# Exponentials and maxima on crossed score banks: VectorE and ScalarE change places halfway

## The chip, the cores and the metric

One core of one Trainium2 chip runs the whole kernel. The metric is the device time in microseconds of one execution, and the time of a kernel is the median of its runs.

## The reference, cut to what matters

A gated block over x of 128 sequences of 64 tokens with 128 channels: a cross attention with 16 heads of 8 channels, and a feed-forward network whose tokens are routed to one of 8 experts. The change lies in the attention's softmax.

```python
def _L0_xattn_ref(q, k, v, W_q, b_q, W_k, b_k, W_v, b_v, W_o, b_o):
    qh = _split_heads(q @ W_q + b_q)
    kh = _split_heads(k @ W_k + b_k)
    vh = _split_heads(v @ W_v + b_v)
    scores = jnp.einsum('bhqd,bhkd->bhqk', qh, kh) / jnp.sqrt(jnp.asarray(D_K, qh.dtype))
    probs = jax.nn.softmax(scores, axis=-1)
    ctx = jnp.einsum('bhqk,bhkd->bhqd', probs, vh)
    ...
x = x + jnp.tanh(g_xattn[0]) * _L0_xattn_ref(_layernorm(x), ctx_1024, ctx_1024, ...)
x = x + jnp.tanh(g_ffn[0]) * _L0_ffn_ref(_layernorm(x), ...)
```

## The kernel before, in words

The attention is a pipeline written out by hand. A unit is 128 tokens (two sequences); there are 64 units (NU), and four of them share a load, a projection and a turn of the inputs. One loop over slots k = 0 to 75 stands in each engine's program, and in slot k every engine does the stages of several units at once: scores for the maxima of unit k-4 (LAG1), scores for the exponential of unit k-10 (LAG2), values of unit k-11 (LAGV), output projection of unit k-12 (LAGO). With j = k % 4 and s = k // 4, every fourth slot has the same extra work. The engines meet only through semaphores.

The scores stand in one PSUM tile sc of four banks, one bank for each of four groups of heads (t). Columns 0 to 255 of each bank hold the scores that VectorE takes the maxima of (bf16 products, `scores1`, L1162 to L1170), columns 256 to 511 those that ScalarE exponentiates (float32 products from which the maxima of that earlier pass have been taken away by the matmul of MD and usel, `scores2`, L1143 to L1160). There is one sc, so a slot's scores can be written only after the slot before has been read: `scores(k)` waits for pt_ok (the exponentials of the slot before) and mx_ok (its maxima), `peaks(k)` for mx_ok.

TensorE's order in a slot is: scores2 (L1150, L1157), scores1 (L1167), values (L1232, which wait for nv_ok of the unit before), output projection (L1244, which waits for ot_ok), and then what j asks for: in slot j = 0 four transposes of x (L1319), four of the context (L1266), two small ones (L1325, L1327); in j = 1 the keys (L1273); in j = 2 logits (L1256) and queries (L1337, called the wqp matmul); in j = 3 logits and the V projection (L1344).

VectorE's order in a slot is: two reductions of the maxima (L1012), the first over banks 0 and 1 (signals mxa_ok), the second over banks 2 and 3 (mx_ok); the transpose TV (L1021, waits for pv_ps, which the output projection of the slot signals), the residual (L1000), reciprocal (L1027), a statistic (L735), NV (L1032, signals nv_ok), another statistic (L727), the transpose OT (L1039, ot_ok), in j = 1 also L740 and the logits (L811), and in most of the slots from 24 on a step of the routing.

ScalarE's order in a slot is: the two exponentials (L614 over banks 0 and 1, L616 over banks 2 and 3, which signals pt_ok), then the copies that j asks for (j = 0: xT L629, cT L575, mS L663; j = 1: kb L581 and two kT L588; j = 2: qb L644, Qf L647; j = 3: two V copies L656 and xwT L668), and last the squares of the residual (L543, an activation and a read of its accumulator). The first exponential waits for s2_ps (its scores), mxa_ok and pv_ps (its output buffer), the second for mx_ok. So the two engines pass through the banks in one order, ScalarE one step behind VectorE, and never read one bank at the same time.

A second loop of 71 tiles runs the experts behind the attention; nothing in it is touched.

Of the kernel before, what the change touches and what calls it, by code (L numbers as in the profile page):

```python
# [6 lines left out]
ACT = mybir.ActivationFunctionType  # L7
# [16 lines left out]
NU = N // P  # L24
# [16 lines left out]
LAG1, LAG2, LAGV, LAGO = 4, 10, 11, 12  # L41
# [22 lines left out]
def gated_block(nc, x, ctx_in, g_xattn, g_ffn, W_q, b_q, W_k, b_k, W_v, b_v, W_o, b_o, w_red, wg, W1, b1, W2, b2, out):  # L64
    es = ExitStack()
    with es:
# [3 lines left out]
        def pb(name, shape, dt=F32):  # L70
            return es.enter_context(nc.psum_tensor(name, shape, dt))

        def sem(name):
            return es.enter_context(nc.semaphore(name))
# [93 lines left out]
        sc = pb("sc", [P, RT, 512])  # L168
# [22 lines left out]
        qd_in = [sem(f"qd_in{i}") for i in range(3)]  # L191
        md_ok = sem("md_ok")
        imask_ok, par_ok, bkp_ok = sem("imask_ok"), sem("par_ok"), sem("bkp_ok")
        s1_ps, mxa_ok, mx_ok, mT_ps, mS_ok, s2_ps, pt_ok = (sem(n) for n in ("s1_ps", "mxa_ok", "mx_ok", "mT_ps", "mS_ok", "s2_ps", "pt_ok"))
        pv_ps, val_ps, tv_ok, rec_ok, nv_ok, ot_ok, x1_ok = (
            sem(n) for n in ("pv_ps", "val_ps", "tv_ok", "rec_ok", "nv_ok", "ot_ok", "x1_ok"))
        gsq_ok, gve_ok, g_pay, xw_ps, xwT_ok, xwt_ps, lgx_ok = (
# [13 lines left out]
        def pv_turn(k):  # L211

            return k - LAGV + 1
# [280 lines left out]
        def _(act):  # L494
# [8 lines left out]
            def permuted(w, wp):  # L503
                nc.scalar.activation(wp[:, :].rearrange("p (t d i) -> p t d i", t=RT, d=DK),
                                     w[:, :].rearrange("p (t i d) -> p t d i", t=RT, d=DK), ACT.Copy).then_inc(perm_ok, 1)

            def permuted_biases():
                for i in range(2):
                    b_ = nc.scalar.activation(browp[:, i, :].rearrange("o (t d i) -> o t d i", t=RT, d=DK),
                                              brow[:, i, :].rearrange("o (t i d) -> o t d i", t=RT, d=DK), ACT.Copy)  # L510
                b_.then_inc(brow_ok, 1)
# [3 lines left out]
            def bias_columns():  # L515
                act.wait_ge(bcol_ps, 1)
                nc.scalar.mul(b16[:, 0:1], m2[:, 0:1], ISC)
                nc.scalar.activation(b16[:, 1:2], m2[:, 1:2], ACT.Copy).then_inc(b16_ok, 1)
                act.wait_ge(b16_ok, 1)
                act.wait_ge(par_ok, 1)  # L520
                nc.scalar.activation(bkp[:, :], par[:, :], ACT.Copy, scale=b16[:, 1:2]).then_inc(bkp_ok, 1)
                act.wait_ge(bkp_ok, 1)
# [33 lines left out]
            def gate_weights_end():  # L556
                act.wait_ge(wc_ps, 1)
                nc.scalar.activation(wc[:, 0:NE], m2[:, 0:NE], ACT.Copy).then_inc(wc_ok, 1)

            def turned_weights():  # L560

                act.wait_ge(wt_ps, 1)
                nc.scalar.activation(wt[:, :, :].rearrange("p a c -> p (a c)"), pv[:, P:3 * P], ACT.Copy).then_inc(wt_ok, 1)
# [7 lines left out]
            def turned_context(s):  # L571
                act.wait_ge(cT_ps, s + 1)
                if s >= 1:
                    act.wait_ge(v_ps, s)
                nc.scalar.activation(cT[:, :], m1[:, :], ACT.Copy).then_inc(cT_sb, 1)  # L575
# [29 lines left out]
            for k in range(SLOTS):  # L605
                s, j = k // CU, k % CU
                n = k - LAG2
                if 0 <= n < NU:
                    act.wait_ge(s2_ps, n + 1)
                    act.wait_ge(mxa_ok, min(k - LAG1 + 1, NU))  # L610
                    if n >= 2:
                        act.wait_ge(pv_ps, pv_turn(n - 2 + LAGV))
                    pt = PT[n % 2][:, :, :].rearrange("p (t i) q -> p t (i q)", t=RT)
                    nc.scalar.activation(pt[:, 0:2], sc[:, 0:2, 256:512], ACT.Exp)  # L614
                    act.wait_ge(mx_ok, min(k - LAG1 + 1, NU))
                    nc.scalar.activation(pt[:, 2:4], sc[:, 2:4, 256:512], ACT.Exp).then_inc(pt_ok, 1)  # L616
                if k == 7:
                    gate_weights_end()
                if k == 0:
                    turned_context(0)  # L620
                    permuted(wq, wqp)
                    permuted_biases()
                    bias_columns()
                    keys(0)
                if j == 0 and s < NC:
                    act.wait_ge(xT_ps, s + 1)
                    if s >= 2:
                        act.wait_ge(xw_ps, s - 1)
                    nc.scalar.activation(xT[s % 2][:, :], m0[:, :], ACT.Copy).then_inc(xT_sb, 1)  # L629
                if k == 0:  # L630
                    keys_turned(0)
                    act.wait_ge(w_in, 16 * NWI)
                    nc.scalar.activation(tg[:, :], gx[:, :], ACT.Tanh)
                    nc.scalar.activation(tgf[:, :], gf[:, :], ACT.Tanh).then_inc(tg_ok, 1)
                if j == 0 and 1 <= s < NC:
                    turned_context(s)
                if j == 1 and 1 <= s < NC:
                    keys(s)
                    keys_turned(s)
                if j == 2 and s < NC:  # L640
                    act.wait_ge(q_ps, s + 1)
                    if s >= 2:
                        act.wait_ge(s1_ps, CU * (s - 1))
                    nc.scalar.activation(qb[s % 2][:, :], m0[:, :], ACT.Identity, bias=b16[:, 0:1], scale=ISC).then_inc(qb_ok, 1)  # L644
                    if s >= 1:
                        act.wait_ge(qd_in[(s - 1) % 3], 16 * HI * ((s - 1) // 3 + 1))
                    nc.scalar.activation(Qf[:, :], m0[:, :], ACT.Identity, bias=b16[:, 0:1], scale=ISC).then_inc(qf_ok, 1)  # L647
                if j == 3 and s < NC:
                    act.wait_ge(v_ps, s + 1)
                    if s < 3:  # L650
                        act.wait_ge(zero_p, s + 1)
                    else:
                        act.wait_ge(pv_ps, pv_turn(CU * (s - 3) + CU - 1 + LAGV))
                    for p in range(2):
                        r = slice(S * p, S * p + S)
                        i = nc.scalar.activation(V[s % 3][r, :, :, DK * p:DK * p + DK].rearrange("p u h d -> p (u h) d"),  # L656
                                                 m1[r, :].rearrange("p (a d) -> p a d", d=DK), ACT.Copy)
                    i.then_inc(v_ok, 1)
                if j == 0 and 2 <= s < NC + 2:
                    act.wait_ge(mT_ps, s - 1)  # L660
                    if s >= 4:
                        act.wait_ge(md_ok, s - 3)
                    nc.scalar.activation(mS[s % 2][:, :], m2[:, 0:P], ACT.Copy, scale=-1.0).then_inc(mS_ok, 1)  # L663
                if j == 3 and 1 <= s < NC + 1:
                    act.wait_ge(xw_ps, s)
                    if s >= 2:
                        act.wait_ge(xwt_ps, s - 1)
                    nc.scalar.activation(xwT[:, :], m2[:, P:2 * P], ACT.Copy).then_inc(xwT_ok, 1)  # L668
                if k == 5:
                    reduced_weights()  # L670
                if k == 6:
                    turned_weights()
                if k == 10:
                    output_logits()
                if k - LAGO - 1 >= 0:
                    squares(k - LAGO - 1)
                if k in gate_at:
                    gate_exp(gate_at[k])
                if k == SLOTS - 3:
                    nc.scalar.activation(warm[:, :], one[:, :], ACT.Gelu)  # L680
                if k == SLOTS - 3:
                    f_turned(0)
                if k == SLOTS - 2:
                    f_gelu(0)
                    f_turned(1)
# [11 lines left out]
        def _(dve):  # L697
# [305 lines left out]
            for k in range(SLOTS):  # L1003
                s, j = k // CU, k % CU
                n = k - LAG1
                if 0 <= n < NU:
                    c, u = n // CU, n % CU
                    dve.wait_ge(s1_ps, n + 1)
                    if c >= 2 and u == 0:
                        dve.wait_ge(mT_ps, c - 1)  # L1010
                    for t, done in ((0, mxa_ok), (2, mx_ok)):
                        nc.vector.tensor_reduce(mx[c % 2][:, t:t + 2, HI * u:HI * u + HI],  # L1012
                                                sc[:, t:t + 2, 0:256].rearrange("p t (i k) -> p t i k", i=HI),
                                                AX_X, ALU.max).then_inc(done, 1)
                n = k - LAGV
# [8 lines left out]
                n = k - LAGV  # L1024
# [403 lines left out]
```

## Time and profile before

| what | value |
|---|---|
| median of 3 runs | 367.36 us (364.79 to 367.79) |
| span of the profiled execution | 445.2 us |
| what lies around the span | not given for this execution |
| PE, DVE, ACT, POOL busy in the span | 354.6, 288.0, 241.2, 260.1 us |
| instructions | 15463 |

The profile is one execution on its own, and its span is 78 us longer than the median of the runs without a profile. Durations of single instructions are taken from it. Busy time is what an engine works; TensorE's matmuls overlap, and their ends are modelled. The attention lasts from the start to some 292 us of the span, the experts from there to the end.

### The profile page before, as it was taken

What the parts mean: (1) busy time and instruction counts of PE and PEld (TensorE: products, weight loads), DVE (VectorE), ACT (ScalarE), POOL (GpSimd) and SP (SyncE); (2) the same over time, 40 slices, a digit from 0 to 9 for tenths busy, and PEclk for the clock granted to TensorE, in tenths of its full rate; (3) what the DMA queues carried; (4) which work ended last, traced back from release to release, by engine and by line L of the source; (5) the groups of instructions that cost most, each with busy time, mean ns of one, the idle gap of its engine ahead of it and who ended that gap; (6) DMA issues with size and microseconds to landing.
All of it is one profiled execution on the core that took longest, in us unless ns stands there. A gap on an engine that the chain in (4) does not pass through costs nothing.

```text
span 445.2 us, 15463 instructions
## 1 busy us (share of the span) xinstructions
PE 354.6 (80%) x5630; PEld 257.0 (58%) x5630; DVE 288.0 (65%) x1031; ACT 241.2 (54%) x604; POOL 260.1 (58%) x413
## 2 busy tenths in 40 slices
PE   4778999999979889889876776768559888878880
PEld 2346566676636556566543545557448667766770
DVE  6968798989848766868853657565435454445440
ACT  3667889888938676777762524443212333333330
POOL 6558465556866945865854444446564656556652
PEclk9989999999969897998995967579685999999997
DMA  5245444333232131221110111401134222222110
GB/s 124 86 134 132 114 122 121 110 99 106 73 93 77 58 100 35 93 76 35 52 54 28 45 35 49 113 28 41 51 98 115 84 83 81 79 69 77 49 36 4
DMA packets 47157, 34.01 MB, mean 76 GB/s; under 512 B 9800, under 2 KB 42955, under 8 KB 47083
## 3 DMA queue, kind: packets, MB, share of 16 engines
q1 hardware_dynamic: 42440, 23.90, 19.5%
q0 software_dynamic: 4352, 9.00, 6.0%
q8 instruction: 46, 0.75, 0.7%
q14 instruction: 27, 0.22, 0.2%
q10 hardware_dynamic: 292, 0.13, 0.1%
HBM read 17.13 MB, written 10.04 MB: 61 GB/s over the span
## 4 chain that ended last, share of the span: by engine, by line
PE 59%; DVE 14%; issue 12%; ACT 4%; another core or an unknown queue 4%; SPq 2%; DMA 1%; POOL 1%; DVEq 1%; POOLq 0%; ACTq 0%
PE sc L1286 10%; PE m L1384 8%; PE pv L1232 8%; PE sc L1157 5%; PE pv L1244 4%; PE m L1337 4%; PE m L1344 3%; PE sc L1167 3%; PE sc L1150 3%; DVE mx L1012 3%; PE m L1256 2%; PE sc L1278 2%; PE m L1381 2%; PE m L1273 2%
## 5 line engine op out<-in xcount | busy, mean ns | idle before, releaser
L1012 DVE TENSOR_REDUCE mx<-sc 128x8 f32<-128x512 f32 x128 | 82.2, 683 | 45.5 <-PE sc L1167 23.6
L489 POOL DMA_INDIRECT out<-fo,rr x71 | 72.0, 1014 | 58.7 <-DVE fo L1083 39.4
L1232 PE MATMUL pv<-PT,V 128*32 128x64 f32 x2048 | 55.7, 233 | 25.0 <-issue 20.0
L416 POOL DMA_INDIRECT records<-XR,pos x64 | 63.4, 990 | 17.0 <-issue 16.8
L1083 DVE SCALAR_TENSOR_TENSOR fo<-m,rr 128x128 f32<-128x128 f32 x71 | 24.8, 350 | 66.3 <-PE m L1384 55.2
L614 ACT ACTIVATE PT<-sc 128x512 f32<-128x512 f32 x64 | 38.1, 596 | 53.3 <-issue 27.5
L1232 PEld LDWEIGHTS pv<-PT,V 128*32 128x32 f32 x2048 | 39.0, 115 | 39.3 <-issue 32.2
L1286 PE MATMUL sc<-fxT,w1s 128*128 128x128 f32 x284 | 50.2, 304 | 5.6 <-DVE w1s L991 3.0
L1384 PE MATMUL m<-w,fgT 128*128 x284 | 52.9, 313 | 0.1
L459 POOL TENSOR_TENSOR MD<-mS,imask 128x256 bf16<-128x256 bf16 x16 | 9.8, 612 | 70.4 <-ACT mS L663 70.4
L602 ACT ACTIVATE fgT<-sc 128x256 f32<-128x256 f32 x71 | 27.2, 383 | 41.7 <-PE sc L1286 29.5
L1286 PEld LDWEIGHTS sc<-fxT,w1s 128*128 128x128 f32 x284 | 41.0, 208 | 11.6 <-issue 7.8
L1157 PE MATMUL sc<-Qd,kT 32*128 32x128 f32 x1024 | 46.3, 288 | 1.2 <-issue 1.2
L596 ACT ACTIVATE fxT<-sc 128x128 f32<-128x128 f32 x70 | 19.4, 277 | 49.8 <-PE sc L1278 25.2
L1384 PEld LDWEIGHTS m<-w,fgT 128*128 128x128 f32 x284 | 40.5, 206 | 2.2 <-issue 0.2
L1157 PEld LDWEIGHTS sc<-Qd,kT 32*128 32x128 f32 x1024 | 39.4, 201 | 2.8 <-issue 2.7
L1021 DVE STREAM_TRANSPOSE TV<-pv 128x256 f32<-128x256 f32 x64 | 28.3, 441 | 18.6 <-remote 13.1
L616 ACT ACTIVATE PT<-sc 128x512 f32<-128x512 f32 x64 | 38.2, 597 | 0.0
L1278 PE MATMUL sc<-ident,fx 128*128 128x128 f32 x70 | 21.4, 306 | 13.3 <-DVE fx L975 9.2
L1244 PE MATMUL pv<-wox,OT 128*128 128x137 f32 x108 | 29.0, 350 | 1.4 <-issue 1.4
L1150 PEld LDWEIGHTS sc<-MD,usel 32*128 32x128 bf16 x256 | 6.5, 92 | 36.7 <-ACT PT L616 23.7
L543 ACT ACTIVATE dev<-XR 128x128 f32<-128x128 f32 x64 | 25.8, 404 | 1.5 <-issue 1.3
(216 smaller groups left out, 735.3 us busy)
## 6 DMA issues: line engine op xcount, KB each, us to landing
rr<-records SPq DMA_DIRECT2D x71, 72.0 KB, 1.9
XC<-in_x SPq DMA_DIRECT2D x16, 256.0 KB
C<-in_ctx SPq DMA_DIRECT2D x16, 256.0 KB
Qd<-Qf SPq DMA_DIRECT2D x64, 64.0 KB
Kd<-kb SPq DMA_DIRECT2D x64, 32.0 KB
w<-in_L_ffn_W SPq DMA_DIRECT2D x16, 128.0 KB, 2.9
out<-fo,rr POOLq DMA_INDIRECT x71
w1l<-in_L_ffn_W SPq DMA_DIRECT2D x8, 128.0 KB, 3.9
```

Source lines behind the costliest of these rows:

```text
L416: nc.gpsimd.indirect_dma_start(out=records, out_offset=bass.IndirectOffsetOnAxis(ap=pos[:, u:u + 1], axis=0), in_=XR[:, u, :], in_offset=N ...
L489: nc.gpsimd.indirect_dma_start(out=out_rows, out_offset=bass.IndirectOffsetOnAxis(ap=rr[q][:, R_ID:R_ID + 1].bitcast(U32), axis=0), in_=fo ...
L614: nc.scalar.activation(pt[:, 0:2], sc[:, 0:2, 256:512], ACT.Exp)
L616: nc.scalar.activation(pt[:, 2:4], sc[:, 2:4, 256:512], ACT.Exp).then_inc(pt_ok, 1)
L1012: nc.vector.tensor_reduce(mx[c % 2][:, t:t + 2, HI * u:HI * u + HI], sc[:, t:t + 2, 0:256].rearrange("p t (i k) -> p t i k", i=HI), AX_X, ...
L1021: nc.vector.transpose(TV[:, :, :].rearrange("p a r -> p (a r)"), pv[:, 0:2 * P]).then_inc(tv_ok, 1)
L1157: m = nc.tensor.matmul(sc[:, t, 256 + P * b:256 + P * b + P].rearrange("p (i q) -> p i q", i=2), kT[c % 3][r, u, b, :, :].rearrange("r l k ...
L1232: last = nc.tensor.matmul(pv[32 * t:32 * t + 32, P * b:P * b + P].rearrange("p (h i q) -> p i h q", h=2, i=2)[:, i], vf[:, at:at + 32], PT ...
L1244: last = nc.tensor.matmul(attn_out(k), OT[no % 2][:, :], wox[:, :], start=True, stop=True, skip_group_check=True)
L1278: nc.tensor.transpose(rows_turned(k), fx[k % 2][:, :], ident[:, :]).then_inc(f_tr, 1)
L1286: i = nc.tensor.matmul(sc[:, 2 + p, P * m:P * m + P], w1s[p][:, P * m:P * m + P], fxT[p][:, :], start=True, stop=True, skip_group_check=True)
L1384: i = nc.tensor.matmul(o, fgT[p][:, m, :], w2[:, bass.ds(e, 1), m, :].rearrange("p o c -> p (o c)"), start=False, stop=(m == HH - 1), skip ...
```

## The change

ScalarE takes the exponential of banks 2 and 3 first. It waits for the slot's maxima scores to be written (s1_ps) where it waited for the first maxima, and it signals a new semaphore, pth_ok. VectorE takes the maxima of banks 0 and 1 at that time and, before those of banks 2 and 3, waits for pth_ok. ScalarE takes banks 0 and 1 after mxa_ok and then signals pt_ok. VectorE's new wait stands in the slots from LAG2 (10) on, up to the last one with maxima (67).

```diff
-        s1_ps, mxa_ok, mx_ok, mT_ps, mS_ok, s2_ps, pt_ok = (sem(n) for n in ("s1_ps", "mxa_ok", "mx_ok", "mT_ps", "mS_ok", "s2_ps", "pt_ok"))
+        s1_ps, mxa_ok, mx_ok, mT_ps, mS_ok, s2_ps, pth_ok, pt_ok = (
+            sem(n) for n in ("s1_ps", "mxa_ok", "mx_ok", "mT_ps", "mS_ok", "s2_ps", "pth_ok", "pt_ok"))
...
                     act.wait_ge(s2_ps, n + 1)
-                    act.wait_ge(mxa_ok, min(k - LAG1 + 1, NU))
+                    act.wait_ge(s1_ps, min(k - LAG1 + 1, NU))
                     if n >= 2:
                         act.wait_ge(pv_ps, pv_turn(n - 2 + LAGV))
                     pt = PT[n % 2][:, :, :].rearrange("p (t i) q -> p t (i q)", t=RT)
-                    nc.scalar.activation(pt[:, 0:2], sc[:, 0:2, 256:512], ACT.Exp)
-                    act.wait_ge(mx_ok, min(k - LAG1 + 1, NU))
-                    nc.scalar.activation(pt[:, 2:4], sc[:, 2:4, 256:512], ACT.Exp).then_inc(pt_ok, 1)
+                    nc.scalar.activation(pt[:, 2:4], sc[:, 2:4, 256:512], ACT.Exp).then_inc(pth_ok, 1)
+                    act.wait_ge(mxa_ok, min(k - LAG1 + 1, NU))
+                    nc.scalar.activation(pt[:, 0:2], sc[:, 0:2, 256:512], ACT.Exp).then_inc(pt_ok, 1)
...
                     for t, done in ((0, mxa_ok), (2, mx_ok)):
+                        if t == 2 and k >= LAG2:
+                            dve.wait_ge(pth_ok, k - LAG2 + 1)
                         nc.vector.tensor_reduce(mx[c % 2][:, t:t + 2, HI * u:HI * u + HI],
```

## Rows read from the trace of the kernel before

**Rows 1.** The page: busy time of TensorE, and the granted clock in 40 slices

```profile
PE 354.6 (80%) x5630; PEld 257.0 (58%) x5630; DVE 288.0 (65%) x1031; ACT 241.2 (54%) x604; POOL 260.1 (58%) x413
PEclk9989999999969897998995967579685999999997
```

**Rows 2.** Windows: stretch, length, busy time (instructions) by engine, clock, DMA share, GB/s

```profile
66.25:79.00 12.75, 12.58 (x307) 8.75 (x305) 11.34 (x40) 11.58 (x27) 6.93 (x16) 1.00 0.40 121
79.00:92.58 13.58, 12.90 (x305) 8.88 (x302) 12.84 (x47) 11.65 (x27) 8.95 (x18) 1.00 0.35 96
105.47:118.55 13.08, 12.64 (x307) 8.76 (x304) 11.84 (x43) 11.72 (x28) 8.24 (x17) 1.00 0.31 95
120.00:240.00 120.00, 100.55 (x1994) 66.70 (x1985) 81.90 (x279) 79.03 (x183) 80.05 (x130) 0.89 0.21 68
```

**Rows 3.** Timeline of TensorE, one period: start, length, line, tiles, idle before

```profile
66.25 0.29 PE L1150 MATMUL sc<-MD,usel 32*128 32x256 bf16 x4
...
69.27 0.29 PE L1150 MATMUL sc<-MD,usel 32*128 32x256 bf16 x4
...
71.11 1.02 PE L1273 MATMUL m<-cT,wkp 128*128 128x512 f32 x2
72.31 0.29 PE L1150 MATMUL sc<-MD,usel 32*128 32x256 bf16 x4 [0.17 <-ACT PT L616]
...
73.22 0.65 PE L1232 MATMUL pv<-PT,V 128*32 128x64 f32 x32
...
74.58 1.12 PE L1337 MATMUL m<-xT,wqp 128*128 128x512 f32 x2
75.64 0.29 PE L1150 MATMUL sc<-MD,usel 32*128 32x256 bf16 x4
...
78.99 0.29 PE L1150 MATMUL sc<-MD,usel 32*128 32x256 bf16 x4
```

**Rows 4.** Timeline of ScalarE in the same period

```profile
66.36 1.20 ACT L656 ACTIVATE V<-m 64x512 f32<-64x512 f32 x2 [0.49 <-PE m L1344]
...
68.05 0.19 ACT L543 ACTIVATION_READ_ACCUMULATOR dev<-XR 128x1 f32 x1
68.14 0.59 ACT L614 ACTIVATE PT<-sc 128x512 f32<-128x512 f32 x1
...
70.52 0.22 ACT L543 ACTIVATION_READ_ACCUMULATOR dev<-XR 128x1 f32 x1
...
72.17 0.69 ACT L581 ACTIVATE kb<-m,b 128x512 bf16<-128x512 f32 x1
...
74.47 0.60 ACT L614 ACTIVATE PT<-sc 128x512 f32<-128x512 f32 x1
```

**Rows 5.** Timeline of VectorE, slots 0 and 1 of the same period

```profile
67.30 1.29 DVE L1012 TENSOR_REDUCE mx<-sc 128x8 f32<-128x512 f32 x2 [0.56 <-PE sc L1167]
68.50 0.44 DVE L1021 STREAM_TRANSPOSE TV<-pv 128x256 f32<-128x256 f32 x1
...
69.39 0.29 DVE L1032 TENSOR_TENSOR NV<-TV,pv 128x128 f32<-128x128 f32 x1
...
69.80 0.29 DVE L1039 STREAM_TRANSPOSE OT<-NV 128x128 f32<-128x128 f32 x1
70.33 1.29 DVE L1012 TENSOR_REDUCE mx<-sc 128x8 f32<-128x512 f32 x2 [0.24 <-PE sc L1167]
```

**Rows 6.** Chain of waits, slot 1, and the keys of a later slot: start, length, what

```profile
70.74 0.37 issue
...
97.62 0.86 PE m L1273 x2
```

**Rows 7.** VectorE's reductions from 60 to 120 us: shortest, median, longest

```profile
L1012 DVE TENSOR_REDUCE mx<-sc x37: 675/683/693, 60.6 to 119.6; 128x8 f32<-128x512 f32 x37
```

**Rows 8.** Waits from 120 to 245 us: total, times, longest

```profile
DVE mx L1012 <- remote: 21.7, 7, 6.7
```

**Rows 9.** Chain of waits after a pause of TensorE: the wqp matmul

```profile
201.35 2.01 PE m L1337 x2
```

## The prediction

> **What bounds the kernel now.** I read the views from wide to narrow. The page gives TensorE 80% of the span, and its clock row shows full speed with dips only in the middle [rows 1]. The windows then separate the stretches: in the period from 66.25 to 79.00, TensorE is busy 12.58 of 12.75 us at clock 1.00, while VectorE is busy 11.34 and ScalarE 11.58 [rows 2]. TensorE binds, but neither of the others has much more than 1 us of air in four slots. Any wait that is added to one of them must be looked at against that air. Last I read the timelines of this period engine by engine [rows 3 to 5]. In what follows a slot's time zero is the start of its sel matmul (L1150): 66.25, 69.27, 72.31, 75.64 and 78.99, so slots j = 0 to 3 last 3.02, 3.04, 3.33 and 3.35 us [rows 3]. In slots 0, 2 and 3 TensorE runs through. Only into slot 2 does it wait, for the second exponential of slot 1 (L616): the wait of 0.17 stands on its row at 72.31 [rows 3]. The chain of waits shows why: at 70.74 ScalarE has nothing to do for 0.37 us before its exponential at 71.11 [rows 6]. What it waits for is the first maxima: the reduction that starts at 70.33 takes 0.69 and ends at 71.02 [rows 5, 7].
>
> **The change part by part.** (a) ScalarE's first exponential no longer waits for the first maxima, only for the scores. (b) VectorE's second reduction (banks 2 and 3) gets a wait for ScalarE's exponential of the same banks. (c) The banks change order, with the same number of instructions: two reductions, two exponentials, same shapes. So only the waits count. A released engine starts 0.08 us after the end it waited for (71.02 to 71.11), TensorE 0.05.
>
> Gain of (a): ScalarE is free for the exponential 0.09 after its accumulator read starts (68.05 to 68.14 [rows 4]; the accumulator's row of each slot is the last of its squares). In slot 1 that is 70.52 + 0.09 = 70.61, half a microsecond before 71.11. The other slots are bound by TensorE, so only slot 1 can pay. TensorE's own work there ends at 71.11 + 0.86 = 71.97 by the chain's figure for L1273 [rows 6], or at 72.07, if its row, which ends at 72.13, reaches 0.06 past the next start as that of L1337 does (75.70 against 75.64 [rows 3]); slot 2 starts at 72.31. So 0.24 to 0.34 us in four slots is all that (a) can give.
>
> Price of (b): it falls where ScalarE comes late. Slot 0: the V copies start 0.11 after zero (66.36), the exponential 1.89 after (68.14), although the scores are there at 1.05 (reduction at 67.30). Slot 2: the kb copy at 72.17 is followed by two kT copies and the squares, and the exponential starts at 74.47, 2.30 later. In both, VectorE now waits before its second reduction, which goes 0.61 behind the first, and everything behind it in its queue waits too: the transpose TV, the residual, NV, OT. TensorE needs NV for the next slot's values (L1232, 0.91 after zero) and both maxima for its next scores. Slot by slot, with the new waits:
> Slot 0: exponential of banks 2 and 3 from 1.89 to 2.49, second reduction 2.57 to 3.25, next scores at 3.30 instead of 3.02: +0.28.
> Slot 1: TV starts 0.59 after that reduction, at 3.16, NV ends 1.18 later (69.39 + 0.29 - 68.50 [rows 5]), at 4.34, which is 1.04 in slot 1. The values start at 1.09 instead of 0.91. TensorE's work then ends at 2.70 or 2.80 (71.97 or 72.07) plus that 0.18, so 2.88 to 2.98; I take 2.92. VectorE comes free at 1.4 (OT ends 1.59 after TV), reduces to 2.69, and the exponentials end at 2.77 with the hop to TensorE 2.82. Slot 1 lasts 2.92 instead of 3.04: -0.12. Here (a) pays, less what the late NV takes back.
> Slot 2: the keys now end later than ScalarE needs them, so kb starts 0.20 after zero (their last half runs on past TensorE's next start), the exponential at 2.50 to 3.10, the second reduction 3.18 to 3.86, next scores at 3.91 instead of 3.33: +0.58.
> Slot 3: NV ends at 3.18 + 0.59 + 1.18 = 4.95, that is 1.04, values at 1.09, so 3.35 + 0.18 = 3.53: +0.18.
> Together 13.66 instead of 12.75, +0.91 a period.
>
> The bounds of (b): if ScalarE always were ready at the scores, nothing; the kb and V copies late by the whole amount in every slot would be 0.58 each, 2.3 a period. No row shows either, so the value is the replay's. The wait as an instruction is not shown either. Nearest is TV, which has a wait that is met early and still starts at 68.50, before the pair of reductions ends at 67.30 + 1.29 = 68.59 [rows 5]: nothing is the lower end. The upper is the overlap of 0.08 lost in 52 slots, 4 us; I take nothing, as TV shows.
> The Trainium skill, "VectorE: DVE Perf Modes", section "The DRAIN you can't avoid", says that the next operation does not start until the pipeline has emptied, and that a semaphore costs nothing extra. By it nothing would be added for the wait either, but every pair would last 1.37. The trace shows 1.29: the second starts 0.61 after the first, whose length is 0.68 to 0.69 [rows 5, 7]. The measurement decides, and the sum stays.
>
> **The sum.** The wait (b) stands in slots 10 to 67. Slots 16 to 67 have the full ScalarE load: 13 periods, 13 x 0.91 = 11.8 us. The three windows of whole periods last 12.75, 13.58 and 13.08 [rows 2]; the excess over 12.75 is routing work of VectorE and short pauses in which VectorE is the late one anyhow. Of the mean excess (0.39) I let a third be covered by the new wait, 0.13 a period over ten periods: 1.3 off. That leaves +10.5. Against the profiled execution (445.2 us of span, what lies around it isn't shown) less remains: between 120 and 245 us VectorE stands before its reduction for 21.7 us in 7 long waits on nothing the profile can name [rows 8], and behind them ScalarE isn't late. They swallow slot 2's 0.58 seven times, 4 us: some 452 us. The median of the runs without a profile, 367.36, is 78 us lower than that span, so most of those pauses are not in it, and the full term holds: 367.4 + 10.5 = 377.9, say 378.
>
> **The rivals.**
> The gain alone: faster. If VectorE's late second reduction is absorbed (TensorE's next scores not behind it), slot 1 gives up 0.27 a period, 13 x 0.27 = 3.5 us, 363.9. It decides at the point where ScalarE's exponential can start by 1.43 in slot 0 and 1.74 in slot 2: then NV still ends 0.05 before the next values want it (1.43 + 0.68 + 0.59 + 1.18 = 3.88, against 3.02 + 0.86). For it: VectorE is idle 0.56 before slot 0's reduction. Against it: 68.14 and 74.47 are set by copies that the change leaves alone. A chance of 0.13.
> Most of the price is hidden: pauses as in the later part of the trace also stand in the runs without a profile, and only slot 0's 0.28 less slot 1's 0.12 and slot 3's share remains, some 0.25 a period: 13 x 0.25 = 3.3, 370.6. For it: the stretch from 120 to 240, where TensorE is busy 100.55 of 120 [rows 2]. Against it: the 78 us. A chance of 0.12.
> The clock falls. After pauses the wqp matmul takes 2.01 [rows 9] for what is 1.06 at full clock (74.58 to 75.64 by the next start). A slot of 3.33 us would grow by the same ratio of 1.9, by 3.0; if one slot in four ran so, 13 x 3.0 + 10.5 = 49.5 us more, 417; a few of them give 385 to 395. Against it: the new pauses are 0.2 to 0.5 us, and the waits of 0.17 and the like leave the clock at 1.00 through the first three windows [rows 2]. A chance of 0.05.
> The Trainium skill, "TensorE: Matmul & The Clock Gate", section "A second HAM failure mode: psum-queue depth-cycling", says that small idle times between groups of matmuls can be frequent enough to make the clock swing between its two levels. By it the change would be at up to 417 and not at 378; in the windows at hand the clock stays at full speed.
>
> **How the numbers follow.** The forecast has 0.70 (its own range 373 to 383, from the 0.13 and 0.58 terms), the three rivals 0.13, 0.12 and 0.05. The range of 369 to 385 takes in the second rival and leaves out the gain and the clock. Faster or slower counts from 1%, about what a measurement can tell here (363.7 and 371.0). The gain case lies on that edge, 0.05 faster and 0.08 the same; the hidden case half the same, half slower. So faster 0.05, same 0.14, slower 0.81.
>
> **What would show it.** In a clean period of the changed kernel: slots of 3.3, 2.9, 3.9 and 3.5; the second reduction no longer right behind the first in slots 0 and 2 but 0.9 and 1.5 later than now, released by ScalarE's exponential; VectorE's idle time moved in between the two; TensorE waiting in each new slot for VectorE, where now it waits for L616. Wrong, if the two reductions stay together in slots 0 and 2, if ScalarE's exponential starts in them before 1.43 and 1.74, if a period is under 13, or if the clock row falls in the first 120 us.

## The result

The changed kernel takes 378.58 us (median of 5 runs, 375.49 to 379.61) against 365.99 for the kernel before (five runs, 363.26 to 367.79). The ratio is 1.0325, with a 95% interval of 1.0257 to 1.0394: 12 us slower, where a median of 378 was forecast. Medians take all executions and ratios only those in the faster of two states that any kernel shows, so the two can differ by about a per cent; the profile of the first experiment is of its slowest execution (372.45).

The page of the changed kernel, answering to [rows 1]: busy times, and the granted clock.

```profile
PE 315.5 (84%) x5630; PEld 237.2 (63%) x5630; DVE 289.4 (77%) x1031; ACT 240.7 (64%) x604; POOL 257.4 (69%) x413
PEclk9998999999999999999999999899998999999985
```

Its span is 373.7 us, shorter than the 445.2 of the first profile of the kernel before although the kernel is slower. The long pauses of that first profile belonged to that one execution: a second profile of the kernel before (first experiment) has a span of 369.9, and neither has them. VectorE and ScalarE are busy for 289 and 241 us, as before (288 and 241), and the medians of single instructions are the same (a reduction 0.68 to 0.69, an exponential 0.60), so the instructions did not become longer; what grew is waiting. The clock stays up: the mean granted clock of the five executions is 0.951 to 0.970, and of the eleven of the kernel before in the first experiment 0.947 to 0.974.

Who waited for whom, changed kernel, 66 to 230 us; the columns are total, times, longest:

```profile
DVE mx L1015 <- ACT PT L615: 16.2, 25, 1.1
...
DVE mx L1015 <- PE sc L1170: 2.4, 4, 0.8
PE sc L1153 <- DVE mx L1015: 2.2, 9, 0.3
...
PE pv L1235 <- DVE NV L1035: 1.3, 5, 0.3
```

The first line is new: VectorE stands 16.2 us before its reductions for ScalarE's first exponential (L615). The second is the old wait for the scores, which is nearly gone: what VectorE used to wait for first, it now finds ready. The last two are TensorE held by VectorE's second reduction and by NV, 9 and 5 times and at most 0.3 us; both are new.

Whole stretches, each from the start of slot 16 to that of slot 68, 13 periods: first the changed kernel, then the kernel before in two profiles of the experiments (the second with its squares moved, which changes nothing in the time). Columns as in [rows 2].

```profile
53.69:237.22 183.53, 167.11 (x3943) 116.97 (x3940) 160.04 (x554) 147.56 (x351) 127.78 (x218) 1.00 0.28 85
```

```profile
57.05:232.03 174.98, 162.06 (x3943) 113.94 (x3940) 159.25 (x552) 147.85 (x350) 128.66 (x218) 1.00 0.30 90
```

```profile
51.93:225.48 173.55, 164.00 (x3943) 115.12 (x3941) 159.27 (x552) 148.38 (x349) 128.84 (x218) 0.98 0.30 90
```

These 52 slots take 8.6 to 10.0 us more, with the same work in them (VectorE 160 against 159). The profiled execution of the changed kernel was its fastest, 3.1 us under its median. From slot 68 to the end nothing was lost: 136.5 us in the changed kernel, 137.9 and 137.7 in the others.

The first of the 13 periods, slots 16 to 19, has no routing work in it yet, like the period of [rows 3] from which the forecast was worked out:

```profile
53.69 0.29 PE L1153 MATMUL sc<-MD,usel 32*128 32x256 bf16 x4
...
57.05 0.29 PE L1153 MATMUL sc<-MD,usel 32*128 32x256 bf16 x4 [0.26 <-DVE mx L1015]
...
60.01 0.29 PE L1153 MATMUL sc<-MD,usel 32*128 32x256 bf16 x4
...
62.41 0.60 ACT L615 ACTIVATE PT<-sc 128x512 f32<-128x512 f32 x1
...
63.88 0.29 PE L1153 MATMUL sc<-MD,usel 32*128 32x256 bf16 x4 [0.46 <-DVE mx L1015]
...
67.40 0.29 PE L1153 MATMUL sc<-MD,usel 32*128 32x256 bf16 x4
```

Its slots last 3.36, 2.96, 3.87 and 3.52, together 13.71; 3.30, 2.92, 3.91 and 3.53, together 13.66, were forecast.

A later period of the changed kernel (slots 40 to 43), with routing work in it: timeline, the lines of all three engines that set its course; it answers to [rows 3 to 5]:

```profile
137.78 0.29 PE L1153 MATMUL sc<-MD,usel 32*128 32x256 bf16 x4
137.90 1.20 ACT L657 ACTIVATE V<-m 64x512 f32<-64x512 f32 x2 [0.74 <-PE m L1347]
...
138.84 0.69 DVE L1015 TENSOR_REDUCE mx<-sc 128x8 f32<-128x512 f32 x1
...
139.68 0.59 ACT L615 ACTIVATE PT<-sc 128x512 f32<-128x512 f32 x1
...
140.30 0.69 DVE L1015 TENSOR_REDUCE mx<-sc 128x8 f32<-128x512 f32 x1 [0.77 <-ACT PT L615]
...
141.13 0.29 PE L1153 MATMUL sc<-MD,usel 32*128 32x256 bf16 x4 [0.26 <-DVE mx L1015]
...
141.79 0.29 DVE L1035 TENSOR_TENSOR NV<-TV,pv 128x128 f32<-128x128 f32 x1
...
142.22 0.65 PE L1235 MATMUL pv<-PT,V 128*32 128x64 f32 x32
...
144.20 0.69 ACT L582 ACTIVATE kb<-m,b 128x512 bf16<-128x512 f32 x1 [0.51 <-PE m L1276]
...
144.48 0.29 PE L1153 MATMUL sc<-MD,usel 32*128 32x256 bf16 x4
...
146.50 0.60 ACT L615 ACTIVATE PT<-sc 128x512 f32<-128x512 f32 x1
...
147.13 0.69 DVE L1015 TENSOR_REDUCE mx<-sc 128x8 f32<-128x512 f32 x1 [0.90 <-ACT PT L615]
...
147.96 0.29 PE L1153 MATMUL sc<-MD,usel 32*128 32x256 bf16 x4
...
149.05 0.65 PE L1235 MATMUL pv<-PT,V 128*32 128x64 f32 x32
...
151.52 0.29 PE L1153 MATMUL sc<-MD,usel 32*128 32x256 bf16 x4
```

The slots last 3.35, 3.35, 3.48 and 3.56. The first slot holds the whole story. ScalarE's V copies start at +0.12, after an idle time of 0.74 in which it waited for TensorE's V projection, and its exponential starts at +1.90, behind these copies. VectorE reduced the first two banks from 138.84 to 139.53 and then stood for 0.77 until 140.30, 1.46 behind its first reduction instead of 0.61; TensorE starts the next scores 0.14 after that reduction. One slot later TensorE's values (142.22) start 1.09 after the slot's start instead of 0.91, since NV ended only at 142.08. Slot 42 repeats it with 0.90 before the reduction, slot 43 has the late values again.

In the chain of waits of the same kernel, the one that decides when it ends, TensorE's work is broken by just that sequence:

```profile
138.84 0.25 ACT V L657
...
139.12 0.28 ACT xwT L669
139.40 0.38 ACT dev L544 x2
139.78 0.50 ACT PT L615
...
140.30 0.70 DVE mx L1015
```

### The profile page after: what moved, and what is told of

It reads as the page before. It is cut to its first block, busy times and chain, and to the rows that moved or that the text cites. A ratio compares the mean times of both kernels' runs of the same rounds, so it can differ in the third digit from the quotient of the medians.

```text
span 373.7 us, 15463 instructions
## 1 busy us (share of the span) xinstructions
PE 315.5 (84%) x5630; PEld 237.2 (63%) x5630; DVE 289.4 (77%) x1031; ACT 240.7 (64%) x604; POOL 257.4 (69%) x413
## 4 chain that ended last, share of the span: by engine, by line
PE 56%; DVE 21%; issue 8%; ACT 7%; SPq 2%; POOL 2%; DMA 1%; POOLq 0%; DVEq 0%; ACTq 0%
PE m L1387 10%; PE sc L1289 8%; PE pv L1235 6%; PE sc L1160 5%; DVE mx L1015 5%; PE m L1347 4%; PE pv L1247 4%; PE m L1340 3%; PE sc L1170 3%; PE sc L1153 3%; PE m L1276 2%; DVE TV L1024 2%; PE m L1259 2%; PE m L1384 2%; ACT PT L615 2%
## 5 line engine op out<-in xcount | busy, mean ns | idle before, releaser
L1015 DVE TENSOR_REDUCE mx<-sc 128x8 f32<-128x512 f32 x128 | 84.9, 682 | 26.0 <-ACT PT L615 19.5
L1235 PE MATMUL pv<-PT,V 128*32 128x64 f32 x2048 | 43.8, 223 | 7.8 <-DVE NV L1035 4.3
L1289 PE MATMUL sc<-fxT,w1s 128*128 128x128 f32 x284 | 45.3, 283 | 4.0 <-DVE w1s L992 2.9
L617 ACT ACTIVATE PT<-sc 128x512 f32<-128x512 f32 x64 | 38.4, 599 | 14.2 <-DVE mx L1015 12.6
L1235 PEld LDWEIGHTS pv<-PT,V 128*32 128x32 f32 x2048 | 33.7, 110 | 17.9 <-issue 12.2
L1289 PEld LDWEIGHTS sc<-fxT,w1s 128*128 128x128 f32 x284 | 37.9, 194 | 6.4 <-ACT fxT L597 3.9
L615 ACT ACTIVATE PT<-sc 128x512 f32<-128x512 f32 x64 | 38.0, 594 | 6.1 <-PE sc L1160 5.7
L1160 PE MATMUL sc<-Qd,kT 32*128 32x128 f32 x1024 | 41.2, 274 | 0.0
L1160 PEld LDWEIGHTS sc<-Qd,kT 32*128 32x128 f32 x1024 | 35.4, 188 | 0.0
L1153 PE MATMUL sc<-MD,usel 32*128 32x256 bf16 x256 | 18.9, 278 | 13.2 <-ACT PT L617 7.3
L366 POOL TENSOR_TENSOR rstd<-ve,mhalf 128x4 f32<-128x4 f32 x16 | 16.5, 1031 | 18.5 <-DVE ve L741 18.4
L976 DVE TENSOR_SCALAR fx<-rr 128x127 f32<-128x127 f32 x71 | 28.2, 396 | 0.0
```

The lines of the kernel that those rows point to most:

```text
L976: nc.vector.tensor_scalar(fx[p][:, 0:D - 1], rr[q][:, 0:D - 1], rr[q][:, R_MEAN:R_MEAN + 1], rr[q][:, R_RSTD:R_RSTD + 1], ALU.subtract, AL ...
L1153: nc.tensor.matmul(sc[:, t, 256:512].rearrange("p (b i q) -> p i b q", b=2, i=2), usel[r, u, :, :].rearrange("r l k -> r (l k)"), MD[c % 2 ...
L1160: m = nc.tensor.matmul(sc[:, t, 256 + P * b:256 + P * b + P].rearrange("p (i q) -> p i q", i=2), kT[c % 3][r, u, b, :, :].rearrange("r l k ...
L1235: last = nc.tensor.matmul(pv[32 * t:32 * t + 32, P * b:P * b + P].rearrange("p (h i q) -> p i h q", h=2, i=2)[:, i], vf[:, at:at + 32], PT ...
L1289: i = nc.tensor.matmul(sc[:, 2 + p, P * m:P * m + P], w1s[p][:, P * m:P * m + P], fxT[p][:, :], start=True, stop=True, skip_group_check=True)
```

## The experiments

**The kernel before again.** No edit.

> The kernel before once more, for a profile without the long pauses of the first one and as a measure of noise. Every theory: ratio 1.00, and a clean period of four slots of 12.7 to 13.1 us, which is to be set beside the 13.7 to 14.6 of the changed kernel.

366.35 us, ratio 1.0032 (0.9995 to 1.0069). Its slots 40 to 43, from the timeline:

```profile
138.16 0.29 PE L1150 MATMUL sc<-MD,usel 32*128 32x256 bf16 x4
...
141.19 0.29 PE L1150 MATMUL sc<-MD,usel 32*128 32x256 bf16 x4
...
144.36 0.29 PE L1150 MATMUL sc<-MD,usel 32*128 32x256 bf16 x4
...
147.69 0.29 PE L1150 MATMUL sc<-MD,usel 32*128 32x256 bf16 x4
...
151.04 0.29 PE L1150 MATMUL sc<-MD,usel 32*128 32x256 bf16 x4
```

3.03, 3.17, 3.33 and 3.35, together 12.88, to be set against the 13.74 of the changed kernel. Slot 41 lasts 3.17 here and not the 3.04 of [rows 3]: it has the routing's count matmuls in it, and TensorE has no pause then. That is so in 5 of the 13 slots of this kind; slots 17 and 21 last 3.03 and 3.04.

**VectorE set free.** The early exponential stays; the second reduction reads a zeroed tile in SBUF (`blanks`, whose allocation is left out of the cut below) and waits for nothing, so the maxima of half the heads are left out.

```diff
...
                     for t, done in ((0, mxa_ok), (2, mx_ok)):
-                        if t == 2 and k >= LAG2:
-                            dve.wait_ge(pth_ok, k - LAG2 + 1)
                         nc.vector.tensor_reduce(mx[c % 2][:, t:t + 2, HI * u:HI * u + HI],
-                                                sc[:, t:t + 2, 0:256].rearrange("p t (i k) -> p t i k", i=HI),
+                                                (blanks[:, :, :] if t else sc[:, 0:2, 0:256]).rearrange("p t (i k) -> p t i k", i=HI),
...
```

> The changed kernel, but VectorE's second reduction reads a zeroed SBUF tile instead of score banks 2 and 3 (so those heads' exponentials are taken without their maxima subtracted) and has no wait for the exponential. The early exponential stays, the hold of VectorE goes. Theory H (VectorE held behind a late ScalarE costs it all): faster than before by what slot 1 gives, 0.27 x 13 = 3.5 us, 362 to 364. Rival O (ScalarE's new order, or its handover from half to half, costs by itself): stays near 375.

367.69, ratio 1.0102 (1.0032 to 1.0173). Most of the loss is gone: theory H stands as to the loss, and rival O falls as the main cause. The gain that H counted on here (362 to 364), and the first rival of the prediction with it, isn't there.

**The wait alone, with the reduction on SBUF.** As above, with the two lines of the wait kept.

> As the one before (second reduction on a zeroed SBUF tile), but with the wait for the exponential kept. Theory H: the wait alone brings the whole loss back, 377 to 380. Rival P (both engines reading PSUM at once is slower): the loss is mostly gone, since VectorE's second reduction no longer reads PSUM, 366 to 370.

378.57, ratio 1.0415 (1.0328 to 1.0501). This kernel and the one before it differ in nothing but the wait, and it costs 10.9 us (378.57 - 367.69). The 52 slots from 16 to 67, without the wait and with it, show where:

```profile
55.11:228.42 173.31, 162.52 (x3942) 114.33 (x3940) 158.17 (x551) 145.09 (x351) 127.97 (x218) 1.00 0.30 90
```

```profile
55.05:239.04 183.99, 166.61 (x3943) 116.69 (x3940) 159.95 (x554) 147.28 (x351) 127.89 (x218) 1.00 0.29 85
```

That is 10.7 us, so the cost lies in the slots that have the wait. Rival P falls: that both engines read PSUM at once isn't what costs. Nor is an instruction longer for it: the second reduction's median is 0.69 us on SBUF here and 0.69 on the score banks in the changed kernel, and the exponentials' is 0.60 (rounded) in both. The Trainium skill, "PSUM — Partial Sum Buffer", section "Specifications (TRN2)", says the same: the two can read in parallel at full bandwidth as long as their banks differ.

**The control for both.** The kernel before with the same SBUF tile under its second reduction.

> The kernel before with its second reduction on a zeroed SBUF tile (those heads' exponentials without their maxima subtracted): the control for the two runs with that edit. Every theory: 364 to 367, since the reduction keeps its length within some 0.05 us; if it is shorter on SBUF, the runs with it have to be read against this one.

367.34, ratio 1.0026 (0.9976 to 1.0076). The tile itself changes nothing that can be measured, so the kernel with VectorE free is 0.8% over its control, with intervals that overlap; in the 52 slots the two take 173.31 and 172.95.

**Crossing in slots 0 and 2.** `crossed(k)` is `k >= LAG2 and k % CU in (0, 2)`; where it is false, ScalarE takes its exponentials as in the kernel before (these lines are left out of the cut below) and VectorE doesn't wait.

```diff
-                    act.wait_ge(s1_ps, min(k - LAG1 + 1, NU))
+                    if crossed(k):
+                        act.wait_ge(s1_ps, min(k - LAG1 + 1, NU))
+                    else:
+                        act.wait_ge(mxa_ok, min(k - LAG1 + 1, NU))
...
-                        if t == 2 and k >= LAG2:
-                            dve.wait_ge(pth_ok, k - LAG2 + 1)
+                        if t == 2 and crossed(k):
+                            dve.wait_ge(pth_ok, sum(crossed(m) for m in range(k + 1)))
```

> The crossing only in slots with k % 4 = 0 and 2, the old order in 1 and 3. Theory H: slot 0 +0.28, slot 2 +0.58, slot 3 +0.18 as before; slot 1 begins its reductions late, at 1.4, and has the old three steps behind them, so it ends at 1.40 + 0.78 + 0.55 + 0.60 + 0.05 = 3.38 instead of 3.04, +0.33. Together 1.37 a period, 13 x 1.37 = 17.8 less some 1.3 that was hidden anyhow: 380 to 384, slower than the full change with twice as many crossings. Rival W (each new wait has a like price): half the loss, 372.

385.42, ratio 1.0513 (1.0412 to 1.0614). Half the crossings cost more than all of them, as the slot arithmetic of theory H says, a little over its range. Its split is only partly right: the medians of the 13 slots of each kind are 3.29, 3.73, 3.60 and 3.72, where 3.30, 3.38, 3.91 and 3.53 were counted on. Rival W falls.

**Crossing in slot 0 alone.** The same with `(0,)`.

> The crossing only in slots with k % 4 = 0. Theory H: slot 0 +0.28 and, as its three old steps start late, slot 1 +0.2 to +0.33: 13 x 0.5 to 0.6 = 6.5 to 8 us over before, 371 to 374, with nothing changed in slots 2 and 3. Rival W (each new wait has a like price): 3 us, 369.

376.85, ratio 1.0302 (1.0256 to 1.0348): some 11 us, more than the 6.5 to 8 expected. Its profiled execution was its fastest (373.47), and there the 52 slots take 180.89, only 5.9 and 7.3 us over the two profiles of the kernel before; so in these slots the expectation nearly held, and where the rest of the median lies isn't shown. But single slots go far beyond the arithmetic. Slots 32 and 33 from its timeline:

```profile
107.67 0.29 PE L1164 MATMUL sc<-MD,usel 32*128 32x256 bf16 x4
...
110.34 0.69 DVE L1026 TENSOR_REDUCE mx<-sc 128x8 f32<-128x512 f32 x1 [0.93 <-ACT PT L622]
...
111.18 0.29 PE L1164 MATMUL sc<-MD,usel 32*128 32x256 bf16 x4 [0.43 <-DVE mx L1026]
...
112.46 0.21 DVE L900 TENSOR_REDUCE col<-ey 128x12 f32<-128x96 f32 x1
...
113.11 1.28 DVE L1026 TENSOR_REDUCE mx<-sc 128x8 f32<-128x512 f32 x2
...
114.43 0.60 ACT L628 ACTIVATE PT<-sc 128x512 f32<-128x512 f32 x1
...
115.08 0.29 PE L1164 MATMUL sc<-MD,usel 32*128 32x256 bf16 x4 [0.87 <-ACT PT L628]
```

Slot 0 takes 3.51. Slot 1 takes 3.90, where +0.33 had been allowed over 3.04: VectorE comes to its reductions at 113.11, 1.93 after the start, because a routing step (L900 to L902) stands behind the delayed chain, and two exponentials still follow. In the profile of the first experiment the same slot takes 3.20. In such a slot the routing work, which I had taken as something that hides the wait, adds to it; in slot 37, which takes 4.51 in that profile, this kernel takes 4.17, and there the wait is hidden.

**Crossing in slot 1 alone.** The same with `(1,)`.

> The crossing only in slots with k % 4 = 1, the old order in the others. Theory H: ScalarE is free early there, TensorE's gap of 0.24 goes, 13 x 0.24 = 3.1 us faster than before, 362 to 364. Rival W (each new wait has a like price, 12.6 us over four kinds of slot): a quarter of the loss, 369.

Ratio 0.9959 (0.9889 to 1.0029), median 368.26 of ten runs from 362.02 to 370.52: no gain can be told, and no loss. Neither the 362 to 364 of theory H nor the 369 of rival W is borne out by the ratio. The 52 slots take 174.26, against 174.98 and 173.55 in the kernel before. TensorE's slot 1 does get shorter and slot 2 longer: medians of 2.96 and 3.66, against 3.17 and 3.33.

**Slot 1 crossed, and the squares taken out of the way.** In the same slots (k up to 67) the squares go behind the next exponentials.

```diff
+                if k - LAGO - 2 >= 0 and later(k - 1):
+                    squares(k - LAGO - 2)
                 if k == 7:
                     gate_weights_end()
...
-                if k - LAGO - 1 >= 0:
+                if k - LAGO - 1 >= 0 and not later(k):
                     squares(k - LAGO - 1)
```

> The crossing only in slots with k % 4 = 1, and in the same slots (up to k = 67) the squares moved behind the exponentials of the next slot. Theory G (what slot 1 gains is given back in slot 2, because keys, kb, two kT, squares and two exponentials on ScalarE follow one another and reach past TensorE's own 3.33): with the squares out of that chain slot 2 is back at 3.33 instead of 3.66, slot 1 stays at 2.95, a period of 12.66 against 12.89, 13 x 0.23 = 3 us faster than before, 362 to 363. Rival (slot 2 is late for VectorE's sake, not ScalarE's): slot 2 stays at 3.5 to 3.7, time 365 to 367.

367.31, ratio 1.0001 (0.9965 to 1.0036). Theory G falls, its rival holds. Slots 33 and 34 from the timeline:

```profile
111.73 0.29 PE L1169 MATMUL sc<-MD,usel 32*128 32x256 bf16 x4
...
112.96 1.45 DVE L1031 TENSOR_REDUCE mx<-sc 128x8 f32<-128x512 f32 x2
...
114.53 0.29 PE L1169 MATMUL sc<-MD,usel 32*128 32x256 bf16 x4
...
115.35 0.28 DVE L1051 TENSOR_TENSOR NV<-TV,pv 128x128 f32<-128x128 f32 x1
...
115.78 0.44 PE L1251 MATMUL pv<-PT,V 128*32 128x64 f32 x17 [0.27 <-DVE NV L1051]
```

Slot 1 is down to 2.80. But VectorE, whose queue shows no idle time here, ends NV at 115.63, and TensorE's values start 1.25 after the slot's start instead of 0.91: 0.34 given back. In such a slot VectorE is as much the bound as TensorE. With the squares moved or not, every slot 1 of 2.79 to 2.82 has a slot 2 of 3.66 or more behind it, so the crossing did not get TensorE's pause of 0.24 back.

**The squares later, in the changed kernel and in the kernel before.** First in all slots:

> The changed kernel with ScalarE's squares of the residual (L543) moved from the end of a slot to behind the exponentials of the next. ScalarE comes to its exponentials 0.39 us earlier, and nothing else changes. Theory H: slot 0 has room again (second reduction ends at 2.86, before 3.02), slot 2 ends at 3.53 instead of 3.91: a period of 12.98, 0.23 over the one before, 13 x 0.23 = 3 us: 367 to 371. Rivals O, P and W: nothing changes, 378.

> The same move of the squares in the kernel before. There ScalarE's exponential in slot 1 waits for the maxima and in slots 0 and 2 has time. Every theory: no change, 365 to 367. It is the control for the run with the changed kernel.

378.02, ratio 1.0347 (1.0246 to 1.0447), and 369.32, ratio 1.0109 (1.0031 to 1.0187). Both expectations missed, and the first result by itself is what rivals O, P and W foretold; but the control changed too. In the 52 slots the changed kernel became 3.5 us shorter (180.01 against 183.53), and from slot 68 to the end it takes 140.6 us and its control 140.2, where 136.5 and 137.7 stood above. The chain of waits of the first shows a new piece at the end of the attention:

```profile
252.15 0.39 ACT dev L544 x2
...
252.89 1.05 POOL XR L403
...
253.97 0.19 DVE ex L878
```

The moved squares are late for the last group's routing: GpSimd's power waits for them, VectorE's L878 for GpSimd, and the experts' first tiles for VectorE. So the move was done again for slots up to 67 only:

> The changed kernel with the squares behind the next exponentials in slots up to 67 only, in their old place behind that. In the run that moved them in all slots the attention became 3.5 us shorter and the time didn't. If the end of the attention took it back (the two last squares stand there in front of the experts' first work): 374 to 376. If the shift costs elsewhere: 378.

> The same in the kernel before: control. If the end of the attention took it: 365 to 367 where the move in all slots gave 369.

373.90, ratio 1.0189 (1.0151 to 1.0227), and 366.06, ratio 0.9998 (0.9965 to 1.0031). The control is back, and in the changed kernel a reordering that only lets ScalarE arrive sooner takes off more than a third of the loss. Slot 40 of it, where ScalarE comes 0.40 sooner and VectorE waits 0.38 instead of 0.77:

```profile
138.62 0.29 PE L1158 MATMUL sc<-MD,usel 32*128 32x256 bf16 x4
...
140.75 0.69 DVE L1020 TENSOR_REDUCE mx<-sc 128x8 f32<-128x512 f32 x1 [0.38 <-ACT PT L618]
...
141.64 0.29 PE L1158 MATMUL sc<-MD,usel 32*128 32x256 bf16 x4
```

The slot lasts 3.02, as in the kernel before. What remains is 6.9 us (0.0189 x 367), where the slot arithmetic would leave 3: the medians of slots 1, 2 and 3 are 3.32, 3.68 and 3.52, as in the changed kernel (3.32, 3.68, 3.53), and only slot 0 came back. No version can be told to be faster than the kernel before.

## Why the prediction was right, point by point

- **VectorE held behind a late ScalarE is the cause.** Shown from three sides: the wait alone costs 10.9 us between two kernels that differ in nothing else, and their 52 slots differ by 10.7; without it the loss is gone up to 1%; and with ScalarE 0.4 us earlier it falls from 3.25% to 1.89%.
- **The slots without routing.** In slots 16 to 19 every slot is within 0.06 of the forecast and the period within 0.05 (13.71, forecast 13.66): slot 0 with its exponential at 1.89, slot 1 shorter (2.96), slot 2 with its exponential at 2.40 (forecast 2.50), slot 3 with its values at 1.08. This is the mechanism as it was worked out, and not luck in the sum. The slots with routing are another matter.
- **Slot 0, +0.28.** Measured +0.32 in slot 40: 3.35 against 3.03. The exponential stood at 1.90 (forecast 1.89).
- **Slot 3, +0.18.** Measured +0.21 in slot 43: 3.56 against 3.35, with the values at 1.09 as forecast.
- **Slot 1, -0.12.** Right in slots 17 and 21 (2.96 and 2.79, against 3.03 and 3.04), wrong in its sign in most slots behind them: +0.18 in slot 41, and +0.15 in the medians of the 13 slots (3.32 against 3.17). Two things fail there. In slots like 41 TensorE's own count matmuls fill the pause, so the late values lengthen the slot by their 0.18. In slots like 33 routing steps stand behind OT, and "VectorE comes free at 1.4" fails: the reductions start 1.93 after the slot's start.
- **Slot 2, +0.58.** Measured +0.15 in slot 42, because the longer slot 1 lets the kb copy start at 144.20, 0.28 before slot 2, and not 0.20 after its start: the exponential came at 2.02 instead of 2.50. This slot is not the usual one: the medians are 3.68 against 3.33, +0.35. In slot 34, which lasts 3.68, the kb copy also starts early, and it is NV, late from slot 33, that holds the values until 1.26 instead of 0.91. The errors in slots 1 and 2 have opposite signs: the pair came out at +0.33 in slots 41 and 42 and +0.50 in the medians, where +0.46 was forecast. That the two nearly cancel was luck.
- **The sum.** 10.5 was forecast, 11.8 less 1.3 for cover; the windows give 183.53 - 174.98 = 8.6 to 183.53 - 173.55 = 10.0, the medians 12.6 in all. So in the slots themselves there was cover, and more of it than the 1.3. Set against the profile of the first experiment, seven of the 13 periods (from slots 16, 28, 32, 40, 44, 52 and 56) grew by 0.83 to 0.98, and three (from 24, 36 and 64) by -0.40 to 0.11; what covers the wait in these three wasn't looked into. Part of the closeness of 378.58 to 378 is luck, since the sum is a little too high for the slots and the median holds some 3 us more. Where these lie isn't shown. A place where executions differ is the time before slot 16: it lasts 57.1 us (granted clock 0.85) and 51.9 (0.97) in the two profiles of the kernel before that are shown above, and 53.7 (0.97) in that of the changed kernel.
- **The wait as an instruction.** Taken as nothing, and nothing shows: where it is met early, in slots 17 and 41, the pair of reductions lasts 1.25, against 1.29 before.
- **The overlap of two VectorE instructions.** The prediction read the Trainium skill, "VectorE: DVE Perf Modes", section "The DRAIN you can't avoid", as if every pair had to last 1.37. The same section adds that a following instruction which is not held starts earlier, so the 0.61 between the reductions doesn't contradict it. The sum didn't use it.
- **The profiled execution, 452 us.** Wrong: it took 375.49, with a span of 373.7. I had carried over pauses that were that first execution's own. That the medians would be free of them was right.
- **The rivals.** The gain alone, 363.9: even with VectorE free, and with slot 1 alone crossed, there is no gain to measure. The exponentials of slots 0 and 2 started at 1.90 and 2.02 and not before the 1.43 and 1.74 that this rival needed. The hidden price (370.6): no, since the long pauses that were to hide it are not in the later profiles. The clock: 1.00 in the stretch of 183.53 us, with pauses of TensorE for VectorE of up to 0.46 us (before slot 19, above). The swing between the two clock levels that the Trainium skill describes ("TensorE: Matmul & The Clock Gate", section "A second HAM failure mode: psum-queue depth-cycling") didn't come with pauses of this size.
- **The signs.** The second reduction was to come 0.9 and 1.5 later behind the first in slots 0 and 2. It came 0.85 later in slot 40 (1.46 less 0.61) and 0.99 in slot 42, and 1.23 in slot 18.

## What to carry to other kernels

A wait that makes two engines change places halfway holds the earlier one for as long as the later one is late, and everything in its in-order queue with it. Before adding one, write down for each kind of slot when both engines really arrive, not how busy they are on average. And a pause of the busiest engine is worth its length only if no other engine runs without a gap through the same slots: look there for the engine that has no idle time before any of its instructions.

## What the runs showed of the hardware that I had not expected

How fast a release arrives depends on who gives it to whom. VectorE to TensorE took 0.14 to 0.15 us (reduction ends 140.99, scores start 141.13; NV ends 115.63, values start 115.78), the same in all 17 places between 50 and 240 us where the changed kernel's timeline shows TensorE waiting for VectorE's second reduction or NV. ScalarE to TensorE took 0.05 (115.03 to 115.08) and 0.06 to 0.12 in the eight such places of the changed kernel, VectorE to ScalarE 0.09 (71.02 to 71.11, in the prediction), ScalarE to VectorE 0.03 (140.27 to 140.30) to 0.04. I had used 0.08 for the engines and 0.05 for TensorE; the difference is most of what slot 0 was off.
